# Adding expert results into four per-token sums in memory, instead of storing six rows a token

## What is computed

```python
x = x + xattn(layernorm(x), ctx)        # x (16, 256, 128), 16 heads of 8
x = x + ffn(layernorm(x))

def ffn(x):                              # 4096 tokens of width 128
    shared = (silu(x @ sg.T) * (x @ su.T)) @ sd.T
    scores = sigmoid(x @ gate_w.T) + gate_bias            # 64 experts in 8 groups
    masked = scores * mask_of_the_4_groups_with_the_highest_maxima
    topk_w, topk_i = top_k(masked, 6)
    comb   = scatter(topk_w / topk_w.sum(), topk_i)       # (T, 64)
    h      = silu(einsum('th,eih->eti', x, eg)) * einsum('th,eih->eti', x, eu)
    routed = einsum('eti,ehi,te->th', h, ed, comb)
    return shared + routed
```

## Time and profile before

| | |
|---|---|
| device time, median of 3 runs | 1052.22 us |
| lowest and highest of the 3 | 1044.32 and 1057.37 us |
| profiled execution, span from first to last instruction | 819.3 us |
| median less that span | 232.9 us |
| stage 1, up to the last scatter to `pages` | 0 to 405.8 us |
| stage 2, first quad load to last scatter's end | 407.6 to 757.1 us |
| stage 3 | 757.1 to 819.3 us |
| busy in the span | PE 66%, POOL 67%, DVE 59%, ACT 43% |

### The profile page before, as it was taken

The page is one execution under the profiler, slowest core; times in us unless marked ns, Lnnn a source line. Parts: engine busy times, 40 slices in busy tenths (PEclk is TensorE's granted clock), DMA queues, the critical chain, the costliest instruction groups (busy, mean ns, idle before and its releaser), DMA issues.

```text
span 819.3 us, 13516 instructions
## 1 busy us (share of the span) xinstructions
PE 542.2 (66%) x2966; PEld 449.3 (55%) x2966; DVE 481.1 (59%) x2095; ACT 348.6 (43%) x999; POOL 545.5 (67%) x669
## 2 busy tenths in 40 slices
PE   0599887788787777631088788887778888881000
PEld 0377666667666666530066666676667777661000
DVE  2225999999999999886133333333333333330798
ACT  1456666565666665511144344444444434441000
POOL 2312688888888888877627777778777777877000
PEclk9968787686777777755579888878887777885555
DMA  4222323233333332411132222333333333310884
GB/s 143 105 101 101 125 99 101 99 98 100 100 100 97 101 101 99 145 46 46 56 102 68 66 69 78 102 101 99 97 100 102 103 103 99 101 56 2 294 270 152
DMA packets 82733, 84.61 MB, mean 103 GB/s; under 512 B 22310, under 2 KB 68658, under 8 KB 82704
## 3 DMA queue, kind: packets, MB, share of 16 engines
q1 hardware_dynamic: 64016, 56.67, 23.4%
q0 software_dynamic: 14336, 25.52, 9.3%
q10 hardware_dynamic: 4352, 2.10, 0.9%
HBM read 39.49 MB, written 48.92 MB: 108 GB/s over the span
## 4 chain that ended last, share of the span: by engine, by line
PE 13%; POOL 12%; issue 11%; DVE 8%; DMA 6%; ACT 3%; POOLq 1%; DVEq 0%; ACTq 0%; SPq 0%
POOL results L449 10%; DVE routed L945 5%; PE bank_s L964 5%; PE bank_o L964 4%; DMA results<-y_s,codes 4%; PE bank_s L960 2%; ACT y_s L592 1%; PE bank_r L964 1%; POOL pages L398 1%; DVE h_t L923 1%; DMA pages<-payload,place_i 1%; PE bank_q L960 1%; POOL spare L447 1%; DVE xb L948 1%; ACT pxt L460 1%
## 5 line engine op out<-in xcount | busy, mean ns | idle before, releaser
L449 POOL DMA_INDIRECT results<-y_s,codes x256 | 250.1, 977 | 69.0 <-issue 63.7
L398 POOL DMA_INDIRECT pages<-payload,place_i x192 | 190.1, 990 | 54.8 <-issue 53.4
L592 ACT ACTIVATE y_s<-bank_o,scales 128x128 f32<-128x128 f32 x256 | 73.0, 368 | 76.9 <-PE bank_o L964 74.4
L964 PE MATMUL bank_s<-w_gu,pxt 128*128 x512 | 94.9, 343 | 9.6 <-ACT pxt L460 6.6
L964 PE MATMUL bank_o<-w_d,h_t 64*128 x512 | 89.8, 326 | 6.8 <-DVE h_t L923 6.8
L964 PEld LDWEIGHTS bank_s<-w_gu,pxt 128*128 128x128 f32 x512 | 81.0, 240 | 23.8 <-issue 23.6
L907 DVE TENSOR_TENSOR h_s<-bank_s,s_act 128x256 f32<-128x256 f32 x64 | 27.2, 424 | 110.0 <-ACT s_act L602 110.0
L964 PEld LDWEIGHTS bank_o<-w_d,h_t 64*128 64x128 f32 x512 | 76.1, 225 | 19.8 <-issue 19.7
L923 DVE COPY h_t<-bank_q 64x256 f32<-64x256 f32 x128 | 53.9, 421 | 36.5 <-PE bank_q L960 35.6
L964 PE MATMUL bank_o<-v_all,p_t 128*128 (+1 forms) x512 | 71.4, 285 | 0.0
L964 PEld LDWEIGHTS bank_o<-v_all,p_t 128*128 128x128 f32 x512 | 70.7, 221 | 0.3
(11 more groups left out here) (151 smaller groups left out, 1034.9 us busy)
## 6 DMA issues: line engine op xcount, KB each, us to landing
pg<-pages SPq DMA_DIRECT2D x64, 262.0 KB
pages<-empty SPq DMA_DIRECT2D x21, 786.0 KB
w_gu<-results SPq DMA_DIRECT2D x16, 768.0 KB, 4.7
results<-y_s,codes POOLq DMA_INDIRECT x256
pages<-payload,place_i POOLq DMA_INDIRECT x192, 2.4
raw_w<-in_L_ffn_eg_w SPq DMA_DIRECT2D x16, 128.0 KB
raw_w<-in_L_ffn_eu_w SPq DMA_DIRECT2D x16, 128.0 KB
raw_w<-in_L_ffn_ed_w SPq DMA_DIRECT2D x16, 128.0 KB
```

What stands on the lines that cost most here:

```text
L398: pool.indirect_dma_start(out=pages[:, :], out_offset=bass.IndirectOffsetOnAxis(ap=place_i[t][:, k:k + 1], axis=0), in_=payload[t][:, k, : ...
L449: pool.indirect_dma_start(out=results[:, :], out_offset=bass.IndirectOffsetOnAxis(ap=codes[j][:, g:g + 1], axis=0), in_=y_s[j][:, g, :], i ...
L592: scaled = act.activation(y_s[j][:, g, :], bank_o[:, g * D:(g + 1) * D], ACT.Identity, scale=scales[j][:, g:g + 1])
L964: return pe.matmul(dst, w, v, start=True, stop=True)
```

## The change

`results` becomes four arrays of one row a token, 4 x 4096 rows of 512 bytes. The scatter of page g of a quad adds its rows into sum g, so a row's place is its token alone, and the DMA reads the old row, adds and writes. Since a sum must not be read by one scatter while another has yet to write it, each scatter waits for the landing of the scatter of the same g in the quad before (`landed[g]`). The sums are cleared in stage 1 by four DMAs of SP, 2.1 MB each, from a buffer of zeros. Stage 3 loads four rows a token and sums four. Both dummies and their semaphore are gone. An instruction that sets a register (`pool.reg_alu`) stands ahead of each scatter to `results`, and the bound is taken from that register; the scatters to `pages` have a bound only in the loop and there for the first of six.

```diff
@@ buffers and views
-        spare = sb("spare", [P, 1])
-        ys = [w_flat[:, j * 2 * TOPK * D:(j + 1) * 2 * TOPK * D].rearrange("p (t k h) -> p t k h", t=2, k=TOPK)
+        ys = [w_flat[:, j * 2 * QUAD * D:(j + 1) * 2 * QUAD * D].rearrange("p (t k h) -> p t k h", t=2, k=QUAD)
-        ys_v = results.rearrange("(t p k) h -> p t k h", p=P, k=TOPK)
+        ys_v = results.rearrange("(k t p) h -> p t k h", k=QUAD, p=P)
+        clear_v = results.rearrange("(k p s r) h -> k p s (r h)", k=QUAD, p=P, r=QUAD)
@@ SP
+            sp.wait_ge(nothing_ready, 1)
             for b in range(4):
                 load_batch(b)
                 prefill(2 * b)
                 prefill(2 * b + 1)
+                sp.dma_start(clear_v[b:b + 1, :, :, :].rearrange("k p s c -> (k p) s c"),
+                             y_s[0][:, :, :].rearrange("p g h -> p (g h)").unsqueeze(1).to_broadcast(
+                                 [P, B * TOK // P // QUAD, QUAD * D])).then_inc(results_zeroed, 16)
...
-            for j in range(SLOTS):
-                sp.wait_ge(y_out[j], 16 * QUAD * NQ // SLOTS)
+            for g in range(QUAD):
+                sp.wait_ge(landed[g], 16 * NQ)
...
-                    sp.dma_start(ys[j], ys_v[:, bass.ds(n * 2, 2), :, :]).then_inc(ys_in[j], 16)
+                    for t in range(TPB):
+                        sp.dma_start(ys[j][:, t, :, :], ys_v[:, bass.ds(n * TPB + t, 1), :, :].rearrange(
+                            "p t k h -> p (t k) h")).then_inc(ys_in[j], 16)
@@ POOL
-                pool.wait_ge(spared, TPB * n + t)
-                pool.tensor_tensor(spare[:, :], zeros[:, 0:1], zeros[:, 0:1], ALU.add).then_inc(spared, 1)
+                if not isinstance(n, int):
+                    pool.reg_alu(limit, n, PAGES * P - 1, ALU.add)
...
-                        bounds_check=PAGES * P - 1, oob_is_err=False).then_inc(scattered[t], 16)
+                        in_offset=None, bounds_check=None if k or isinstance(n, int) else limit, oob_is_err=False).then_inc(scattered[t], 16)
...
                     pool.wait_ge(code_ready, q + 1)
                     pool.wait_ge(y_ready, q + 1)
-                    pool.wait_ge(spared, q + TPB * B)
-                    pool.tensor_tensor(spare[:, :], zeros[:, 0:1], zeros[:, 0:1], ALU.add).then_inc(spared, 1)
                     for g in range(QUAD):
-                        pool.indirect_dma_start(out=results[:, :], out_offset=bass.IndirectOffsetOnAxis(
+                        if not (first and j == 0):
+                            pool.wait_ge(landed[g], 16 * q)
+                        pool.reg_alu(limit, i, B * TOK - 1, ALU.add)
+                        pool.indirect_dma_start(out=results[:, :], element_offset=g * B * TOK * D, out_offset=bass.IndirectOffsetOnAxis(
                             ap=codes[j][:, g:g + 1], axis=0), in_=y_s[j][:, g, :], in_offset=None,
-                            bounds_check=B * TOK * TOPK - 1, oob_is_err=False).then_inc(y_out[j], 16)
+                            bounds_check=limit, oob_is_err=False, compute_op=ALU.add).then_inc(landed[g], 16)
+            pool.wait_ge(results_zeroed, 16 * QUAD)
@@ ACT, page_result and ahead of the first quad
-                    act.wait_ge(y_out[j], 16 * QUAD * i)
+                    for g in range(QUAD):
+                        act.wait_ge(landed[g], 16 * (i * SLOTS + j - SLOTS + 1))
+            act.wait_ge(results_zeroed, 16 * QUAD)
@@ DVE
+            dve.memset(y_s[0][:, :, :], 0.0).then_inc(nothing_ready, 1)
...
-                        dve.wait_ge(y_out[j], 16 * QUAD * i)
+                        for g in range(QUAD):
+                            dve.wait_ge(landed[g], 16 * (q - SLOTS + 1))
...
-                    dve.wait_ge(ys_in[j], 16 * (i + 1))
+                    dve.wait_ge(ys_in[j], 16 * TPB * (i + 1))
```

More of the change, by code:

```diff
@@ L210, in build @@
         ranks_done, ranks_ready, placed = sem("ranks_done"), sem("ranks_ready"), sem("placed")
-        payload_x, place_ready, code_ready, spared, digits_done, packed = sem("payload_x"), sem("place_ready"), sem("code_ready"), sem("spared"), sem("digits_done"), sem("packed")
+        payload_x, place_ready, code_ready, digits_done, packed = sem("payload_x"), sem("place_ready"), sem("code_ready"), sem("digits_done"), sem("packed")
         scattered = [sem(f"scattered{t}") for t in range(TPB)]
@@ L214, in build @@
         page_in = [sem(f"page_in{j}") for j in range(SLOTS)]
-        y_out = [sem(f"y_out{j}") for j in range(SLOTS)]
+        landed = [sem(f"landed{g}") for g in range(QUAD)]
+        nothing_ready, results_zeroed = sem("nothing_ready"), sem("results_zeroed")
         pxt_done, pxt_ready, gu_done, act_ready, h_ready = sem("pxt_done"), sem("pxt_ready"), sem("gu_done"), sem("act_ready"), sem("h_ready")
@@ L338, in _ @@
         def _(pool):
+            limit = pool.alloc_register("limit")
             pool.memset(ident[:, :], 0.0).then_inc(zeroed, 1)
@@ L362, in _ @@
             for t in range(TPB):
-                pool.iota(payload[t][:, :, CODE].bitcast(I32), [[1, TOPK]], base=t * P * TOPK - TOK * TOPK,
-                          channel_multiplier=TOPK).then_inc(made, 1)
+                pool.iota(payload[t][:, :, CODE].bitcast(I32), [[0, TOPK]], base=t * P - TOK,
+                          channel_multiplier=1).then_inc(made, 1)
             pool.memset(v_all[:, :, :, :], 0.0).then_inc(values_zeroed, 1)
@@ L392, in wait_payload, with scatter @@
                 pool.wait_ge(prefilled, 16 * (n + FILLS_AHEAD))
-                pool.wait_ge(spared, TPB * n + t)
-                pool.tensor_tensor(spare[:, :], zeros[:, 0:1], zeros[:, 0:1], ALU.add).then_inc(spared, 1)
-            def scatter(t, ks=range(TOPK)):
-                for k in ks:
+                if not isinstance(n, int):
+                    pool.reg_alu(limit, n, PAGES * P - 1, ALU.add)
+            def scatter(n, t):
+                for k in range(TOPK):
                     pool.indirect_dma_start(out=pages[:, :], out_offset=bass.IndirectOffsetOnAxis(
-                        ap=place_i[t][:, k:k + 1], axis=0), in_=payload[t][:, k, :], in_offset=None,
-                        bounds_check=PAGES * P - 1, oob_is_err=False).then_inc(scattered[t], 16)
+                        ap=place_i[t][:, k:k + 1], axis=0), in_=payload[t][:, k, :],
+                        in_offset=None, bounds_check=None if k or isinstance(n, int) else limit, oob_is_err=False).then_inc(scattered[t], 16)
             def body(b, side):
@@ L426, in body @@
                     wait_payload(b - 3, 0)
-                    scatter(0)
+                    scatter(b - 3, 0)
                     wait_payload(b - 3, 1)
-                    scatter(1)
+                    scatter(b - 3, 1)
             pool.wait_ge(mv1_done, TPB)
@@ L439, in _, with quads @@
                 body(b, b % 2)
-            def quads(i):
+            def quads(i, first):
                 for j in range(SLOTS):
@@ L445, in quads @@
                     pool.wait_ge(y_ready, q + 1)
-                    pool.wait_ge(spared, q + TPB * B)
-                    pool.tensor_tensor(spare[:, :], zeros[:, 0:1], zeros[:, 0:1], ALU.add).then_inc(spared, 1)
                     for g in range(QUAD):
-                        pool.indirect_dma_start(out=results[:, :], out_offset=bass.IndirectOffsetOnAxis(
+                        if not (first and j == 0):
+                            pool.wait_ge(landed[g], 16 * q)
+                        pool.reg_alu(limit, i, B * TOK - 1, ALU.add)
+                        pool.indirect_dma_start(out=results[:, :], element_offset=g * B * TOK * D, out_offset=bass.IndirectOffsetOnAxis(
                             ap=codes[j][:, g:g + 1], axis=0), in_=y_s[j][:, g, :], in_offset=None,
-                            bounds_check=B * TOK * TOPK - 1, oob_is_err=False).then_inc(y_out[j], 16)
-            with pool.Fori(0, NQ // SLOTS) as i:
-                quads(i)
+                            bounds_check=limit, oob_is_err=False, compute_op=ALU.add).then_inc(landed[g], 16)
+            pool.wait_ge(results_zeroed, 16 * QUAD)
+            quads(0, True)
+            with pool.Fori(1, NQ // SLOTS) as i:
+                quads(i, False)
         @block.scalar
@@ L767, in find_places @@
                 code = payload[t][:, :, CODE].bitcast(I32)
-                chained("code", dve.tensor_scalar(code, code, TOK * TOPK, None, ALU.add))
+                chained("code", dve.tensor_scalar(code, code, TOK, None, ALU.add))
                 after("rank")
@@ L1182 @@
     args.append(nc.dram_tensor("pages", (PAGES * P, PC), F32, kind="Internal").ap())
-    args.append(nc.dram_tensor("results", (B * TOK * TOPK, D), F32, kind="Internal").ap())
+    args.append(nc.dram_tensor("results", (QUAD * B * TOK, D), F32, kind="Internal").ap())
     build(nc, *args)
```

## The result

The changed kernel takes 1086.65 us (median of 4 runs, 1084.6 to 1092.84). The kernel before, timed beside it, takes 1054.8 us (4 runs, 1044.32 to 1062.4). The ratio is 1.0354 [1.0276, 1.0431]: slower, where 1032 us, a gain, were forecast. The time is 1.7 us above the forecast range. Ratios here are made from the faster runs of a kernel alone (of the four before, 1062.4 is left out), so they are not quite the quotients of the medians. The profiled execution has a span of 1091.0 us and a mean granted clock of 0.658.

A forecast was written before the change was run, and what follows sets the result against it. POOL was taken to bound stage 2, DVE stage 3, both being near their limit in stage 1. Terms -6 + 0 + 0 + 0.8 - 14.2 - 1.1 + 1 - 1 = -20.5 took 1052.2 to 1031.7, said as 1032 us; range 1019 to 1085.

The forecast's parts named there:

- The scatter itself: Stage 2, POOL: an adding scatter holds POOL as long as a plain one, 0 us more; bounds 0 to +250 us.
- Rival 1: Stage 2, L449: an adding scatter holds POOL longer; at +0.49 us each the time is 1157 us; chance 0.28.
- the prediction's own sign of being wrong: Stage 2, POOL: the prediction is wrong if a scatter takes over 1.05 us, whatever else holds.
- 232.9 above it; I carry these 232.9 us over unchanged: Whole kernel: median time 1052.22 us against span 819.3; the difference stays, since the change adds no launch work.
- dummies and bounds, both stages: POOL, stages 1 and 2: dropping the dummies gains 6 us in stage 2 and 1 us in stage 1.
- wait for the landing: Stage 2, POOL: waiting for the previous quad's same scatter to land costs 0, with 2.7 us to spare; bounds 0 to +70.
- stage 3, first load and last landing: Around stage 3: shorter reduces -14.2 us, first load done sooner -1.1, last scatter's landing +0.8.
- clearing the sums: Stage 1, SP's queue: four clearing DMAs delay a context load, +1 us; bounds 0 to +5.
- rival 2: Stage 2: a landing of 5.5 us replaces the dummy as limit, period 5.7 us a quad, time 1070 us; chance 0.10.
- Rival 3: Stage 3: transfers bind; at 200 GB/s 10.5 MB take 52 us, time 1044 us; chance 0.03.
- Rival 4: Stages 3 and 1: more is gained, by a 1.3 us reduce and a stage 1 following POOL, 1021 us; chance 0.04.
- rival 5: Whole kernel: landings, clears and new instructions eat the gain, time 1050 us; chance 0.02.

## Why the prediction was wrong

**The step that failed: "The scatter itself. ... I take 0".** That term decided the result. The nearest row for POOL's time, a scatter without an add, was not near: what the add costs follows neither the bytes nor, for most of it, the rows. Measured are +0.575 us for each of 256 scatters, inside the bounds of 0 to 0.98 that the text gave, with the other value taken. Rival 1 came true, at a bit more than its last example of +0.49. Its place was right (L449, now L459), and so was its price on a quiet chip. The scatter of 1.56 us also is the prediction's own sign of being wrong (over 1.05 us). On a quiet chip the sum with this one term put right is 819.3 - 20.5 + 256 x 0.575 = 946, and the span measured is 947.5. The argument against it ("the time hardly depends on what is moved") was true, with 1558 ns for half the bytes too, and beside the point. Its reason, that the time goes into preparing 128 row copies, was not: half of the rows save 76 of 983 ns.

What was weighed against that choice pointed the right way. By the Trainium skill, "GPSIMD Engine Reference", section "When to use GPSIMD", one core of a pair makes the descriptors of the reads and the other those of the writes, and by "DMA: Bandwidth & Descriptors", section "Rules for kernel authors", an accumulate reads its destination and writes it later. From the two together the prediction worked out two descriptors a row for the reading core. The measured price of a row about doubles, from 1.19 to 2.42 ns, which fits that, but no run shows which core does what. And it is 0.16 of the 0.575 us; most of the price, 0.42, comes once an instruction, and nothing that was weighed gives it.

**The second step that failed: "232.9 above it; I carry these 232.9 us over unchanged".** They were not outside the span: the runs here lie 1.8 us above their spans, on either kind of chip. They were the difference between two chips, and lie in stages 1 and 2 as late waits. This is why the loss measured at first is 31.9 us and not 129.6. That the time lay only 1.7 us above the range is luck: one term too low by 147 us met a chip on which, by the profiles below, some 99 us of it are hidden. On the late chip POOL is not what bounds stage 2 of the kernel before. Its 64 quads take 431.5 us, and those of the kernel after 475.2, all of them at POOL's own 7.45 us: the longer scatters fill time in which POOL had waited. So stage 2 grows by 43.7 us there, 142.9 on a quiet chip (332.0 to 474.9), and stage 3 gives back 13.2. These sum to 30.5, near the 31.9 of the medians. But in the same pair stage 1 ends 37 us later (546.9 against 509.7), so that the two spans differ by 67.8 us and not by 31.9. The chip of the result is not on record and can be another than that of the profile of before, whose time there (1025 to 1030) is 25 us under the 1054.8. So stage 2 supports the account, and the sum doesn't prove it. What the change does in stage 1 costs nothing on a quiet chip. In the four profiles on late chips stage 1 ends at 509.7 (before), 528.0 (without dummies), 546.9 (after) and 549.6 (two of four with the add). That the edits lengthen it there is not excluded; the first of these is of chip 0, the second and the last of chip 15, and this stays open.

The other terms, measured on quiet chips:

| term | predicted | measured | from |
|---|---|---|---|
| scatter adds | 0 | +147.2 | 256 x (1.558 - 0.983) |
| dummies and bounds, both stages | -7 | -2.3 | before less the run without dummies |
| wait for the landing | 0 | 0 | gaps stay 0.30 |
| stage 3, first load and last landing | -14.5 | -14.5 | last scatter's end to the end, 62.6 before, 48.1 after |
| clearing the sums | +1 | 0 | stage 1 ends at 404.6, without clearing (and dummies) 405.65, a difference within the spread |

Together they make +130.4, and the medians differ by 129.6. The 0.8 us is closer than the terms are known: the first is the time of POOL, and as a difference of medians it was 143.4. In the fourth row too the sum is more exact than its parts: a batch became 3.42 - 2.57 = 0.85 us shorter, 13.6 in 16, where 14.2 were forecast.

The dummies are worth a third of the forecast. The gap of 0.30 was right, but a scatter to `results` has become 983 ns; that the register does that isn't separated. In stage 1 the 2.9 us of POOL are not handed on, and neither are the 3 us by which the scatters to `pages` became shorter (187.0 us in all without dummies and bounds, 190.3 before): it doesn't end earlier by anything over the spread. A landing takes 2.7 to 3.7 us and was costed at up to 4.5, hidden; the margin has even grown with the period, and rival 2 is excluded. The reduce was put at 1.85 us and takes 1.89. Rival 3 is excluded as well. In stage 3 of the kernel after on the quiet chip a stretch shows the DMA engines full, but only while loads run ahead, and then DVE finds its data ready:

```profile
904.00:920.00 16.00, 0.00 (x0) 0.00 (x0) 14.30 (x13) 0.00 (x0) 0.00 (x0) 0.50 1.03 288
```

Rival 4 had the wrong sign of the total, and rival 5 no loss to speak of.

## What to carry to other kernels

When a stage hangs on one instruction that is issued hundreds of times, a new option of that instruction has to be priced by itself before anything else is: here one argument of the call cost 143 us, ten times the 14 us that all other edits gained together. If a span and a time of the same kernel differ by a fifth, ask which stage is longer in the slower one before a difference is carried over; an engine that seems to set the pace in one profile may have time to spare where the kernel is really timed. And ask of a gain whether its part can be had alone: 9.1 of the 14.5 us of stage 3 were to be had from an idle engine, with no loss elsewhere that shows.

## What the runs showed of the hardware

- An indirect DMA that adds to memory holds GpSimd 1.56 us for 128 rows, one that only writes 0.98; with 64 rows 1.40 and 0.91. With the add 256 bytes a row take as long as 512 (without it that was not tried), and between two scatters lie 0.30 us. The adding one lands 2.7 to 3.7 us after its issue, the other mostly 2.1 to 2.3. It counts one packet for each row and 16, the other 32 with 64 rows and with 128.
- Two kinds of chips: the same kernel takes 820 us on three of them (35 runs of the kernel before beside the experiments, 817 to 823) and 1030 to 1065 on two others (18 runs). Stage 3 lasts as long on both, and so do most instructions of ACT, DVE and POOL. In stage 1 of the kernel before, TensorE is busy 324 us on chip 0 and 270 on chip 10, at a mean granted clock of 0.69 and 0.75; whether that is a cause or follows from the standing still was not separated. Waits between engines end late, by up to 12 us, in stages 1 and 2. In stage 1 of the kernel after, on a late chip, between 200 and 400 us:

```profile
PE bank_s L979 <- ACT p_t L471: 59.8, 6, 12.0
ACT p_t L471 <- remote: 54.5, 5, 12.0
```

ACT stands still up to 12.0 us before a copy, and PE behind it, 5 and 6 times in these 200 us. What it waits for was neither named by the trace nor tried, and each chip was seen on one occasion only, so whether the kind belongs to the chip, and what makes it, stays open.
